# Two graph layers on one core: the entry's norm, loads, scales and splits dealt anew, and the last two bodies in an order of their own

## What is computed

```python
h = relu(layernorm(x))
q, k, v = heads(h @ Wq + bq), heads(h @ Wk + bk), heads(h @ Wv + bv)   # 16 heads of 32
scores = q @ k.T / sqrt(32);  scores[adj == 0] = -inf
x = x + concat(softmax(scores, -1) @ v) @ Wo + bo
h = relu(layernorm(x))
alpha = relu((h @ wq1) @ (h @ wk1).T) * (adj != 0)
x = x + softmax(alpha, axis=1) @ (h @ weight)
```

## Time and profile before

| | |
|---|---|
| time, median of 3 | 1568.2 us (1566.75 to 1570.06) |
| the profiled execution | 1570.8 us |
| its span | 1569.0 us |
| TensorE (PE) busy | 1504.6 us, 96% of the span |
| VectorE (DVE) busy | 1247.9 us, 80% |
| ScalarE (ACT) busy | 1128.3 us, 72% |
| GpSimd (POOL) busy | 1064.8 us, 68% |
| granted TensorE clock, mean | 0.992 of full speed |

### The profile page before, as it was taken

One profiled execution on the slowest core, in us unless ns is written; L12 is line 12 of the kernel. 1 busy time (PEld: TensorE's weight loads), 2 busy tenths in 40 slices (PEclk: granted clock), 3 DMA queues, 4 the chain that ended last, 5 costly groups with the idle time before them and its releaser, 6 DMA issues.

```text
span 1569.0 us, 50846 instructions
## 1 busy us (share of the span) xinstructions
PE 1504.6 (96%) x16561; PEld 1106.7 (71%) x16561; DVE 1247.9 (80%) x4042; ACT 1128.3 (72%) x2477; POOL 1064.8 (68%) x1478
## 2 busy tenths in 40 slices
PE   2889999999999999999999999999999999999996
PEld 1557777777777777777777777777777777777753
DVE  6778888887887878788888878888887888888763
ACT  2567777777777777777777777777777777777761
POOL 2466767777677777767677776777776777777650
PEclk9999999999999999999999999999999999999998
DMA  7647777667667766666776766777676677767760
GB/s 241 135 95 132 133 163 160 152 136 152 138 138 166 160 144 143 144 136 148 166 157 141 152 140 134 154 160 159 135 158 136 133 161 160 153 135 159 125 119 16
DMA packets 656198, 226.28 MB, mean 144 GB/s; under 512 B 611488, under 2 KB 627872, under 8 KB 656160
## 3 DMA queue, kind: packets, MB, share of 16 engines
q1 hardware_dynamic: 636848, 188.57, 59.1%
q10 hardware_dynamic: 19312, 37.23, 8.5%
HBM read 57.94 MB, written 16.78 MB: 48 GB/s over the span
## 4 chain that ended last, share of the span: by engine, by line
POOL 35%; issue 34%; PE 22%; DVE 4%; ACT 2%; DMA 1%; POOLq 1%; SPq 0%; ACTq 0%; DVEq 0%
PE ring L408 18%; POOL wv_raw L1115 16%; POOL heads_out L1149 6%; POOL x L1172 4%; POOL keep L1181 3%; POOL far L1190 3%; POOL xa L1137 1%; PE score L464 1%; PE pv L483 1%; DMA turned<-wv_raw 1%; POOL newton L1133 1%; PE ring L518 1%; PE pv L485 0%; DVE wk_raw L864 0%; DVE tops L785 0%
## 5 line engine op out<-in xcount | busy, mean ns | idle before, releaser
L1115 POOL TENSOR_TENSOR wv_raw<-wk_raw,wv_raw 128x512 f16<-128x512 f32 x512 | 608.0, 1190 | 362.8 <-ACT wv_raw L638 358.5
L625 ACT ACTIVATE wk_raw<-wk_raw,least 128x256 f32<-128x256 f32 x1024 | 459.0, 497 | 6.8 <-DVE least L864 6.8
L864 DVE CUSTOM_DVE_ANT_0 wk_raw<-score,far,undo_score 128x256 f32<-128x256 f32 x1024 | 444.0, 478 | 7.1 <-issue 5.1
L638 ACT ACTIVATE wv_raw<-wk_raw 128x512 f16<-128x512 f32 x512 | 320.5, 626 | 8.6 <-issue 4.5
L483 PEld LDWEIGHTS pv<-val,turned 128*128 128x128 f16 x2048 | 149.7, 97 | 67.4 <-issue 43.9
L483 PE MATMUL pv<-val,turned 128*128 128x65 f16 x2048 | 185.9, 192 | 10.8 <-DMA turned<-wv_raw 7.0
L408 PE MATMUL ring<-wv_hi,h 128*128 128x256 f16 x1024 | 189.3, 273 | 0.0
L408 PE MATMUL ring<-h,wq_hi 128*128 128x256 f16 x1024 | 176.3, 274 | 7.6 <-DVE wk_lo L827 7.6
L1149 POOL TENSOR_TENSOR heads_out<-o_sum,o_rcp 128x64 f32<-128x64 f32 x512 | 153.0, 320 | 42.6 <-DVE o_sum L879 42.6
L485 PE MATMUL pv<-val,turned 128*128 128x33 f16 x2048 | 178.1, 179 | 0.0
L408 PE MATMUL ring<-h,wk_hi 128*128 128x256 f16 x1024 | 176.6, 274 | 0.0
(11 more groups left out here) (151 smaller groups left out, 3570.6 us busy)
## 6 DMA issues: line engine op xcount, KB each, us to landing
xin<-x_dram ACTq DMA_DIRECT2D x32, 512.0 KB, 3.8
out_dram<-xo SPq DMA_DIRECT2D x32, 512.0 KB, 3.7
xa<-x_dram ACTq DMA_DIRECT2D x31, 512.0 KB, 4.2
adj_in<-adj_dram SPq DMA_DIRECT2D x32, 256.0 KB, 2.9
turned<-wv_raw SPq DMA_TRANSPOSE x512, 3.2
adjt_in<-adj_t_dram SPq DMA_DIRECT2D x32, 256.0 KB, 3.1
wq_raw<-wq_dram SPq DMA_DIRECT2D x2, 512.0 KB, 7.0
wk_raw<-wk_dram SPq DMA_DIRECT2D x2, 512.0 KB, 8.6
```

Source lines behind the costliest of these rows:

```text
L625: last = nc.scalar.activation(probs[:, at, q, :], probs[:, at, q, :], ACT.Exp, bias=least[:, at, q:q + 1], scale=-1.0)
L638: nc.scalar.activation(halves[:, at, :, 0, :], probs[:, at, :, :], ACT.Copy).then_inc(hi["p"], 1)
L864: last = nc.vector.tensor_tensor_reduce(out=probs[:, at, q, :], in0=score[u % GROUP][:, q * NODES:(q + 1) * NODES], in1=far[:, q, :], scal ...
L1115: nc.gpsimd.tensor_tensor(halves[:, at, :, 1, :], probs[:, at, :, :], halves[:, at, :, 0, :], ALU.subtract).then_inc(lo["p"], 1)
```

## The change

- **Graph 0's norm** runs on VectorE instead of POOL, ahead of its low half. POOL's `first_normalise` serves graph 1 and later ones.
- **Loads.** wq follows xa at once on SP; wk is issued by ScalarE's queue; the small biases come behind wq, wv behind them.
- **Scales.** `scaled` is signalled before the bias products (which get `bias_ok`). The first halves of qk0 and of wo wait for fewer split parts. The scale of wv is found behind qk0 and the first scores, not between them. Eight small matmuls (`WARM`) run after the first search. The later search becomes two: one for wo and w1, dealt over the places h2_0 and g0, one for wm at hw1 and av0. The merges move to h2_1, g1, hw0, al, and the bias merge to av1.
- **Splits** come in the order wq, wk, wv, wo, w1, wm, at other steps.
- **End.** Body 31 has `DENSE_LAST`: ot0 in step 13, hw1 in step 15, no av; its softmax is in step 14. Body 32 has `DENSE_END`: av of graph 30 (as av2 and av3, ROLE -2) around h2, then g0, g1, al, hw0, hw1, av0, av1, with its own banks. Graph 31's residual is kept in xa instead of x1.

The diff, cut to its core:

```diff
+DENSE_LAST = [[name for name in step if name not in ("av0", "av1", "hw1", "ot0")] for step in DENSE]
+DENSE_LAST[13], DENSE_LAST[15] = DENSE_LAST[13] + ["ot0"], DENSE_LAST[15] + ["hw1"]
+DENSE_END = [[], ["wo0a", "ot1"], ["wo0b", "wo1a"], ["wo1b"], ["av2"], ["h2_0", "h2_1", "av3"],
+             ["g0"], ["g1"], [], [], ["al"], [], ["hw0"], ["hw1"], ["av0"], ["av1"]]
...
+BANK.update(av2=0, av3=0)
+BANK_END = {**BANK, "h2_1": 1, "g1": 1, "hw0": 2, "hw1": 1}
...
+ROLE.update(av2=-2, av3=-2)
 AL_STEP = step_of("al")
+SOFTMAX_STEP, LAST_SOFTMAX_STEP = AL_STEP + 1, AL_STEP + 3
...
-SPARE = [tile(name) for name in ORDER if tile(name) in ("hw0", "hw1", "g0", "g1", "al", "av0")]
+JOBS = {"h2_0": "turn", "h2_1": 0, "g0": "spread", "g1": 1, "hw0": 2, "al": 3, "hw1": "turn",
+        "av0": "spread", "av1": "bias"}
+SPARE = [tile(name) for name in ORDER if tile(name) in JOBS]
+MERGES = [0, 1, 2, 3, "bias"]
+WARM = 8
...
-SPLIT_TURN = ("wq", "wk", "wv", "wo", "wm", "w1")
-TOP_STEP = 5
-LAST_SCALE_STEP = step_of(SPARE[-1])
+TOP_AT = {(-1, 15): (("wo", 0), ("wo", 1)), (0, 3): (("w1", 0),), (0, 4): (("w1", 1),)}
...
-SPLIT_AT = {(0, 14): 6, (0, 15): 7, (1, 2): 8, (1, 3): 9, (1, 6): 10, (1, 7): 11}
+SPLIT_AT = {(0, 8): 6, (0, 9): 7, (0, 10): 8, (0, 11): 9, (0, 15): 10, (1, 1): 11}
...
+        def residual(b):
+            return xa if isinstance(b, int) and b == BATCH - 1 else x1
...
             sp.dma_start(xa[:], x_v[0, :, :, :]).then_inc(xa_in, 16)
+            for half in range(2):
+                load_raw(sp, "wq", half)
             sp.dma_start(bias_q[:], bq).then_inc(small_in, 16)
...
-            for name in LOADS[:EARLY // 2]:
-                for half in range(2):
-                    load_raw(sp, name, half)
+            for half in range(2):
+                load_raw(sp, "wv", half)
...
+                batch = 2 if at < 3 else 3
+                if job == "turn":
+                    turn_tops(batch, dst)
                     return
...
+                if job == "spread":
+                    spread_scale(batch, 2 if batch == 2 else 1, dst)
+                    return
...
-            WEIGHTS_BY = {("qk0", 0): (w_low, 4), ("v0", 0): (w_low, 6), ("wo0", 0): (w_low, 8),
-                          ("g0", 0): (w_low, 10), ("hw0", 0): (w_low, 12)}
+            WEIGHTS_BY = {("qk0a", 0): (w_low, 2), ("qk0b", 0): (w_low, 4), ("v0a", 0): (w_low, 6),
+                          ("wo0a", 0): (w_low, 8), ("g0", 0): (w_low, 12)}
...
                         turn_tops(0, pv)
                         spread_scale(0, 2, pv)
-                    if nxt and not cur and s == step_of("qk0") - 1:
+                        for _ in range(WARM):
+                            nc.tensor.matmul(ring[1][:, 0:P], ident[:], ident[:], start=True,
+                                             stop=True)
+                    if nxt and not cur and s == step_of("qk0"):
                         turn_tops(1, pv)
-                    if nxt and not cur and s == step_of("qk0"):
-                        spread_scale(1, 1, pv)
...
+                    if nxt and not cur and s == SCORE_STEPS[0]:
+                        spread_scale(1, 1, pv)
...
+                    soften = prev and s == (SOFTMAX_STEP if nxt or not cur else LAST_SOFTMAX_STEP)
+                    if soften:
                         second_exponentials(p)
...
-                    if s == AL_STEP + 1 and prev:
+                    if soften and cur:
                         second_high(p)
...
+                    if soften and not cur:
+                        second_high(p)
...
-                    if nxt and not cur and s == step_of("qk0"):
+                    if nxt and not cur and s == SCORE_STEPS[0]:
                         act.wait_ge(scaled, 2)
...
+            for half in range(2):
+                load_raw(act, "wk", half)
             act.wait_ge(const_ok, 2)
...
+                    if isinstance(t, int) and (t, s) in TOP_AT:
+                        for name, half in TOP_AT[t, s]:
+                            raw_top(name, half, ("wo", "w1").index(name))
+                    if cur and not prev and s == 4:
+                        gather_tops(2)
...
-                    if nxt and not cur and s == step_of("qk0") - 1:
+                    if nxt and not cur and s == step_of("qk0"):
                         round_tops(1, 1, pv)
-                    if nxt and not cur and s == step_of("qk0"):
+                    if nxt and not cur and s == SCORE_STEPS[0]:
                         take_scale(1, 2, 1, pv)
...
             for q in range(QT):
                 first_stats(q, 0)
+            y, a, c = rstd[0][:], newton[0][:, 1, :], newton[0][:, 2, :]
+            dve.wait_ge(rooted[0], 1)
+            step(nc.vector.scalar_tensor_tensor(out=a, in0=y, scalar=-1.0, in1=y,
+                                                op0=ALU.mult, op1=ALU.mult))
...
+            for q in range(QT):
+                nc.vector.tensor_scalar(xa[:, q, :], xa[:, q, :], meanvar[0][:, q, 0:1],
+                                        rstd[0][:, q:q + 1], ALU.subtract, ALU.mult
+                                        ).then_inc(normed[0], 1)
...
             find_scale(0, 0, 2, pv)
+            step(nc.vector.tensor_scalar(scale[:, 0:1], scale[:, 0:1], -SCALE, None, ALU.mult))
+            nc.vector.sem_inc(scaled, 1)
             step(nc.vector.tensor_tensor(undo_score[:], undo[:, 0:1], undo[:, 1:2], ALU.mult))
...
-            nc.vector.sem_inc(scaled, 1)
+            nc.vector.sem_inc(bias_ok, 1)
...
-                        if started(p - 1):
+                        if started(p - 1) and cur:
                             pool.wait_ge(final, count(p - 1, 2, 1))
+                        elif started(p - 1):
+                            pool.wait_ge(lo["h1"], count(p, QT, QT - 1))
...
-            first_normalise(0)
             sweep(pool, body)
```

More of the change, by code:

```diff
@@ L113, in started, with deal, bank_of, order @@
     return not (isinstance(graph, int) and graph < 0)
+def deal(t):
+    if isinstance(t, int) and t >= BATCH - 1:
+        return DENSE_LAST if t == BATCH - 1 else DENSE_END
+    return DENSE
+def bank_of(name, b):
+    if isinstance(b, int) and b == BATCH - 1 and ROLE[name] < 0:
+        return BANK_END[name]
+    return BANK[name]
 def bank_before(name, t):
-    at, shift = ORDER.index(name), 0
+    def order(body):
+        return [other for step in deal(body) for other in step if not other.endswith("b")]
+    body, at = t, order(t).index(name)
     while True:
```

146 lines of the change are left out of this document (81 added, 65 removed).

## The result

The changed kernel takes 1573.2 us (median of 9 runs, 1572.5 to 1575.1), the kernel before 1568.2; the ratio is 1.0037, with a 95% interval of 1.0025 to 1.0050. It is slower by 5 to 6 us (5.0 between the medians, 5.8 by the ratio), where I had forecast 9.5 us less. The profiled executions are less far apart, 1572.6 and 1570.8 us: single executions of the kernel before lie between 1563.7 and 1573.4 us, and the profiled one was in the upper part.

What follows compares the result with a forecast made beforehand. TensorE's own work bounds bodies 2 to 30, so only entry and end could move: -3.1 + 2.6 - 5.0 - 4.0 = -9.5 us, giving 1561.3 profiled and 1558.7 as median forecast, range 1549 to 1565.5.

Steps and rivals of the forecast that it cites:

- the entry's -3.1: All before body 0: earlier norm and scale signal, less xa's delay, save 3.1 us (bounds -5 and -1).
- body 0's -5.4 for the single search: Body 0: splitting the scale search removes gaps of 1.9 and 1.3 us and a half-clock stretch costing about 2.2.
- the jams' waits: Body 0: TensorE waits for VectorE's new backlogs, about 1.8 us in step 7 and 0.6, 1.8, 1.8 later.
- late input: Rival, entry: xa comes 2 us or more late, nearly all of the 3.1 goes (-1.0); 1560.8 us, chance 0.12.
- scores at 32.6: Entry: first scores run at 32.6 instead of 36.81 us (-4.2), after VectorE's qk0 low half.
- Body 0: Body 0: 9.0 us added against 5.4 and 1.0 of absorbed waits, so +2.6 us (bounds -1.5 and +4.5).
- (a): Body 0, steps 5 to 7: first merge's VectorE work ahead of v1b delays step 6's sum; TensorE waits about 1.8 us.
- (b): Body 0, splits in steps 8 to 11: VectorE 15.9 against TensorE 12.0 us; waits 0.6, 1.8, 1.8, then clock 2.2.
- splits serial: Rival, body 0 steps 8 to 15: TensorE pays for each split and both searches; +7.2, 1575.4 us, chance 0.06.
- Body 1: Body 1: one VectorE split instead of four leaves few of its 6.8 us of waits; -5.0 us (bounds -6 and -3).
- End: Last two bodies: new order of softmax, av, hw0 and hw1 saves 4.0 us (bounds -7.5 and -1).
- hw1 in step 15 ... gain 0.8: Body 31: earlier softmax gains 0.8 us despite half-clock hw1; 2.4 with a warm clock, -0.3 at the worst.

Runs made afterwards that it cites:

- section 7: Kernel before with norm on VectorE, new end and hw1 in step 14 (0.9975), plus small matmuls around body 0's single search: 0.9985; mended change with two searches: 0.9967.
- sections 2 and 4: Changed kernel (1.0037) with late splits at old places: 1.0017; without wo's maxima: 1.0026; late splits and first merge in step 6: 0.9987; that merge edit alone: 1.0011.
- search_warm: Kernel before with norm on VectorE, new end, hw1 in step 14 (0.9975), plus five and four small matmuls around body 0's single search: 0.9985.

## Why the prediction was wrong

**Where the time went.** Put together from the ratios: ahead of body 0 +1.4; merge out of step 6 and splits together +7.8 (1.0037 to 0.9987: the merge +4.1 to +4.7, the splits +3.1 to +3.8, by the order in which they are taken back); end -1.3; that leaves -2.2 for the search itself in the measured ratio's +5.8, known to 2.7 us and so not clear of nothing. Every term of the sum was too good. Against my figures for the profiled execution (1561.3 forecast, 1572.6 measured) the changed kernel lost 3.6 us ahead of body 0, 3.3 in body 0, 0.9 in body 1, 1.5 in the middle and 2.0 at the end, and its median lies another 3.2 us further off. Two steps failed by their mechanism: the entry's -3.1, of which nothing came, and body 0's -5.4 for the single search with only the jams' waits against it: 2.2 of the 5.4, the clock, lay beside VectorE's lag (section 7), and the merge and the splits in their new places gave back more than the 3.2 of gaps (sections 2 and 4).

**Entry before body 0: forecast -3.1, measured +1.4 by the ratio, +0.4 in the profile.** The price of the norm was right (2.2 forecast, tops 2.3 earlier). xa's delay was forecast as 1.0 and is 1.36, with another queue's load beside it and the engines near their full share. The Trainium skill, "Trainium Kernel Development and Optimization", Key Constraints, has the rule that transfers of several issuers share the engines; the trace agrees, by 1.36 us where I had put 2 as its price. So the rival "late input" has its mechanism half right: the delay was smaller than its 2 us, and yet all of the 3.1 went. Not seen at all was the bias: of the four small transfers moved behind wq, the last is what VectorE's next instruction waits for. And "scores at 32.6" left ScalarE's order out. qk0's high half stands behind `root` of graph 1 in step 10, which waits for VectorE's stats, as before:

```profile
33.36 0.29 ACT L749 ACTIVATE newton<-meanvar,eps 128x2 f32<-128x2 f32 x1 [6.68 <-DVE meanvar L955]
33.89 0.45 ACT L709 ACTIVATE stage<-ring,bias_q 128x256 f16<-128x256 f32 x1
```

So the scores moved only from 36.8 to 35.7, and as wv's scale now comes behind them, its low half started 0.65 us later than before (39.3 for 38.7) instead of 3.0 earlier. By the Trainium skill, "TensorE: Matmul & The Clock Gate", Part 1, activity lifts the low rate; the trace agrees. qk0's first half did run at full clock behind the eight warming matmuls (12 in 1.5 us or less), and this bought nothing, as I had said; 4.1 us of idle time later the scores were at half clock again. The step that failed here is "scores at 32.6 (-4.2)" with what hangs on it: it passed over ScalarE's queue and the bias, and measured -1.1.

**Body 0: forecast +2.6, measured +5.9 in the profile, +8 to +9 against what the two other profiled executions of the old entry take (51.4 and 49.9).** The places of the jams were right. (a) was forecast as 1.8 and is 2.29, so its size was nearly right, by luck: my reason was VectorE's merge work, and without that work the wait stayed at 2.30. The step that failed is that I let the merge's 3.7 us move without asking what they had covered in step 6. (b) was forecast as 0.6, 1.8 and 1.8; the waits are 0.56 with 0.65, 1.96, 2.59, and the clock 2.6 for 2.2. My opening rule, that the clock falls after gaps of about 2 us, held behind 2.59, but not each time: behind 2.29 in the same body it stayed at 1.00. The rival "splits serial" had the right sign and nearly the right total, 1575.4, but by a body 0 of 72.7 us (53.4 + 19.3) that took 59.3: its point of decision, 65 us, was not reached, and the kernel is slower nevertheless. The larger error is on the other side of the sum: -5.4 for the single search. 3.2 of it were gaps, and they went (a gap of 1.96 for the second search came in their place, as (b) had it); 2.2 were the clock, and search_warm shows these 2.2 to be covered by VectorE's lag; and the profile of before had several us of its own in body 0 that no change needed to remove.

**Body 1: forecast -5.0, measured -4.1.** Right; the waits left are 1.13, 0.91 and 0.4.

**Middle bodies: forecast nothing, measured +1.5 from body 2 to body 30.** It lies in bodies 2 and 3, 94.1 instead of 92.1 us, with three waits for transposes, 2.0 us in all and up to 1.4 each, where the kernel before has none. The kernels with the new bodies 0 and 1 have 93 to 95 there, the others 92 to 94. Why these transposes come late stays open.

**End: forecast -4.0, measured -1.3 (-0.8 in the profiles' means, -2.0 in the two profiles shown).** av in the gap (g0 and g1 5.8 for 8.0), the wait before al (1.50 for 1.6 forecast) and the warm last av (2.75 for 4.3) came as written. The failed step is "hw1 in step 15 ... gain 0.8": I had forecast its half clock and the gaps (2.0, 0.9 and 1.1; measured 2.42, 1.64 and 0.68), but not what they add up to: ot1 came 1.1 us later instead of earlier in this profile, 1.7 in the means. With hw1 in step 14 the 80 us of the forecast were reached in the mean.

**The level.** I subtracted from one profiled execution and shifted the result by 2.6. The terms that I read from waits for transposes and from half-clock stretches are those that differ between executions: the same entry took 4.4 us less to body 1's begin in another profile. That the range ended at 1565.5 and left 6% for slower treats these terms as fixed.

## What to carry to other kernels

When a long matmul group is moved, price what it covered where it was, not only what it adds where it goes: here 3.7 us of merge moved by one step opened a wait of 2.3 us and cost 4.1 to 4.7 by the ratios, and removing 1.4 us of VectorE work ahead of the wait left it at 2.30. A half-clock stretch or a gap on one engine is worth its length only if no other engine is late behind it; look for the next wait in line before it enters the sum. And read a kernel's one-time entry from more than one profiled execution, since waits for DMAs and the clock differ there from one to the next.

## What was not expected of the hardware

With nine small matmuls in place of two waits (1.9 and 1.3 us) that otherwise bring the clock to 0.50, it stayed at 1.00, and fell behind the next wait, of 3.8 us (0.79 over 8 us). A wait of 2.29 us was followed by the full clock in one kernel (a merge in 3.67 us) and by a lower one in another (0.68, the same merge in 5.37). After gaps of 1.15 and 1.53 us with one short group between them it had fallen (scores in 1.14 for 0.83 us), although four small matmuls stood right before the scores. Four transfers of 2 to 256 KB issued behind 1 MB of weights landed late enough to hold VectorE 0.76 us, while the engines' share was 1.05 (12 to 13 us).
